# Expert outputs stored to device memory and fetched by row, in place of one-hot combining matmuls

## What is computed

```python
gate, idx = jax.lax.top_k(probs, 2)                    # S = 192 tokens of a group, E = 8
dispatch = jax.nn.one_hot(prio_se, C)                   # C = 60 places for each expert
combine = dispatch * gate_se[..., None]
expert_in = jnp.einsum('gsec,gsd->egcd', dispatch, xg)
h = jax.nn.relu(jnp.einsum('egcd,edf->egcf', expert_in, wi))
expert_out = jnp.einsum('egcf,efd->egcd', h, wo)
out = jnp.einsum('gsec,egcd->gsd', combine, expert_out)
```

## Time and profile before

| | us |
|---|---|
| median of 3 runs | 406.63 (405.19 to 407.81) |
| the profiled execution, its own time | 405.3 |
| its span in the trace | 403.2 |
| TensorE busy | 377.6 (94%) |
| VectorE busy | 196.0 (49%) |
| ScalarE busy | 113.8 (28%) |
| GpSimd busy | 36.7 (9%) |
| window read for the expert stage | 164.0 to 292.8 |

### The profile page before, as it was taken

The page is one execution under the profiler, slowest core; times in us unless marked ns, Lnnn a source line. Parts: engine busy times, 40 slices in busy tenths (PEclk is TensorE's granted clock), DMA queues, the critical chain, the costliest instruction groups (busy, mean ns, idle before and its releaser), DMA issues. The chain is left out here.

```text
span 403.2 us, 8731 instructions
## 1 busy us (share of the span) xinstructions
PE 377.6 (94%) x3760; PEld 269.6 (67%) x3760; DVE 196.0 (49%) x550; ACT 113.8 (28%) x220; POOL 36.7 (9%) x76
## 2 busy tenths in 40 slices
PE   4999999999979998999999999999999999897874
PEld 4989877887867532747566474655776766676574
DVE  4857798765944371114223132302153547967653
ACT  1213245565520333231413213031103123232130
POOL 7002230111020010000000000000011111110100
PEclk9998999999995999999999999999999999996868
DMA  7936960000000000031230303000000000000004
GB/s 283 312 80 200 246 147 2 6 4 3 2 3 0 0 2 0 2 117 29 91 89 30 118 2 119 0 2 0 2 2 0 2 2 1 2 2 2 1 0 117
DMA packets 13426, 20.35 MB, mean 50 GB/s; under 512 B 2954, under 2 KB 9580, under 8 KB 13388
## 3 DMA queue, kind: packets, MB, share of 16 engines
q1 hardware_dynamic: 13388, 19.80, 17.0%
HBM read 18.61 MB, written 1.18 MB: 49 GB/s over the span
## 5 line engine op out<-in xcount | busy, mean ns | idle before, releaser
L604 PE MATMUL banks<-sb_wo_sl,sb_attn_hidT_attn 128*60 128x192 f32 x768 | 64.1, 327 | 0.0
L604 PEld LDWEIGHTS banks<-sb_wo_sl,sb_attn_hidT_attn 128*60 128x60 f32 x768 | 52.9, 133 | 10.8 <-issue 2.4
L1059 ACT ACTIVATE sb_attn_hidT_attn<-banks 128x480 f32<-128x480 f32 x48 | 24.8, 568 | 99.9 <-PE banks L590 99.9
L1493 DVE COPY sb_w_tok_e_out<-banks 60x384 f32<-60x384 f32 x32 | 17.8, 555 | 71.5 <-PE banks L604 71.0
L586 PE MATMUL banks<-sb_tok_xeT,sb_wi_sl 128*128 128x480 f32 x96 | 45.1, 592 | 1.1 <-ACT sb_tok_xeT L1051 1.1
L586 PEld LDWEIGHTS banks<-sb_tok_xeT,sb_wi_sl 128*128 128x128 f32 x96 | 16.3, 189 | 25.4 <-issue 23.5
L1483 DVE TENSOR_TENSOR sb_comb<-sb_cst,sb_slot_of 128x480 f32<-128x480 f32 x12 | 7.8, 654 | 39.4 <-PE banks L219 39.4
L414 PE MATMUL banks<-sb_tok_xeT 128*128 128x193 f32 (+1 forms) x128 | 26.0, 353 | 0.0
L590 PE MATMUL banks<-sb_tok_xeT,sb_wi_sl 64*128 64x480 f32 x96 | 25.8, 615 | 0.0
L414 PEld LDWEIGHTS banks<-sb_tok_xeT 128*128 128x128 f32 (+1 forms) x128 | 22.3, 201 | 3.0 <-issue 2.6
L571 PE MATMUL banks<-sb_onehot_combT,sb_xn 64*64 64x480 f32 (+1 forms) x144 | 21.8, 586 | 0.0
(11 more groups left out here) (203 smaller groups left out, 572.0 us busy)
## 6 DMA issues: line engine op xcount, KB each, us to landing
sb_wo_sl<-in_wo SPq DMA_DIRECT2D x8, 576.0 KB, 4.9
sb_tok_xeT<-in_xin SPq DMA_DIRECT2D x8, 448.0 KB, 6.8
sb_wi_sl<-in_wi SPq DMA_DIRECT2D x8, 288.0 KB, 3.2
sb_wi_sl<-in_wi SPq DMA_DIRECT2D x24, 96.0 KB, 3.2
...
out<-sb_h SPq DMA_DIRECT2D x16, 72.0 KB, 1.8
...
```

The lines of the kernel that those rows point to most:

```text
L604: mm = nc.tensor.matmul(PS[64 * z:64 * z + CAP, 4 + hf, pr * D:(pr + 1) * D], hidT[:, e % 2, f, g * CAP:(g + 1) * CAP], wo_sl[:, q, f], st ...
L1059: nc.scalar.activation(hidT[:, e % 2, f], PS[:, HID_BANKS[(e * (FT // 2) + f // 2) % 2][f % 2], 0:SLOTS], ACT.Relu).then_inc(sem("hidT"), 1)
L1493: ve.tensor_copy(e_out[64 * (e % 2):64 * (e % 2) + CAP, hf * 4 + z:hf * 4 + z + 3:2, e // 2], PS[64 * z:64 * z + CAP, 4 + hf, 0:2 * D].rea ...
```

## The change

The outputs of expert e now go from PSUM to a two-deep SBUF buffer `rows_out`, and SP stores each half to a device memory tensor (`store_rows`, 16 stores of 192 KB). VectorE computes for each token and each of its two choices k the number of the row in that tensor (`find_rows`, 5 operations on up to 192 values a partition; a token that found no place gets a row of zeros). GpSimd waits for the stores and issues 24 indirect DMAs (`fetch_rows`), one for each tile and k, which each bring 128 rows of 768 bytes. VectorE's new `add_experts(j)` adds row times gate to `h`, 6 operations of 128x192 for a group in place of two. All combine tiles, their transposes and copies, and all of `combine` are gone, and with them the waits of later steps on the combining banks. The gates are now one value for each choice. The constant part of the row numbers comes from 8 small memsets on GpSimd at the start.

```diff
-        gate_of = sb("gate_of", [128, TILES, E])
-        turn_space = sb("onehot_combT", [128, TILES * E // 2 * 128])
-        onehot = turn_space[:, 0:2 * NB * E * CAP].rearrange("t (q b s) -> t q b s", q=2, b=NB)
-        combT = turn_space[:].rearrange("s (i e t) -> s i e t", i=TILES, e=E // 2)
-        comb = sb("comb", [128, 2, E, PADCAP])
+        places = sb("places", [128, TILES, 2, E])
+        gate_of = sb("gate_of", [128, TILES, 2])
+        row_e = sb("row_e", [128, 2, 2 * TILES, E])
+        row_f = sb("row_f", [128, 2, 2 * TILES])
+        row_of = sb("row_of", [128, 2 * TILES], U32)
+        row_space = sb("onehot_rows", [128, 2 * TILES * D + 8 * D])
+        onehot = row_space[:, 0:2 * NB * E * CAP].rearrange("t (q b s) -> t q b s", q=2, b=NB)
+        rows_in = row_space[:, 0:2 * TILES * D].rearrange("t (i d) -> t i d", i=2 * TILES)
+        rows_out = row_space[:, 2 * TILES * D:].rearrange("s (q h g d) -> s q h g d", q=2, h=2, g=2)
...
-        e_out = w_space[:].rearrange("s (g e) d -> s g e d", g=PAIRS)
+
+        expert_rows = [nc.dram_tensor(f"expert_rows{hf}", [E * 2 * 128, D], F32).ap() for hf in range(2)]
...
+            def store_rows(e, hf):
+                sp.wait_ge(sem("e_out"), 4 * e + 2 * hf + 2)
+                sp.dma_start(expert_rows[hf].rearrange("(e s g) d -> e s (g d)", e=E, g=2)[E - 1 - e], rows_out[:, e % 2, hf].rearrange("s g d -> s (g d)")
+                             ).then_inc(sem(f"rows_out{e % 2}{hf}"), 16)
+
+            for e in range(NW):
+                load_expert(e)
             for e in range(E):
-                load_expert(e)
+                if e + NW < E:
+                    load_expert(e + NW)
+                store_rows(e, 0)
+                store_rows(e, 1)
...
-            gp.wait_ge(sem("eo_ps"), 2 * E)
+
+            def fetch_rows(j):
+
+                for i in range(NB * j, NB * j + NB):
+                    for k in range(2):
+                        gp.indirect_dma_start(rows_in[:, 2 * i + k], None, expert_rows[j // 2],
+                                              bass.IndirectOffsetOnAxis(ap=row_of[:, 2 * i + k:2 * i + k + 1], axis=0)
+                                              ).then_inc(sem(f"rows_in{i}"), 16)
+
+            gp.wait_ge(sem("row_of"), 1)
+            for hf in range(2):
+                for q in range(2):
+                    gp.wait_ge(sem(f"rows_out{q}{hf}"), 16 * E // 2)
+                for j in range(2 * hf, 2 * hf + 2):
+                    fetch_rows(j)
             gp.memset(o1T[HD:HD + 1, 0], 1.0).then_inc(sem("pads_zero"), 1)
             gp.wait_ge(sem("pads_zero"), 2)
...
-            def turn_comb(i):
-                pe.wait_ge(sem("comb"), i + 1)
-                need(pe, "combT", i - 1)
-                for ep in range(E // 2):
-                    mm = flip(PS[:, 6 + i % 2, ep * 128:(ep + 1) * 128], comb[:, i % 2, 2 * ep:2 * ep + 2].rearrange("t e c -> t (e c)"))
-                mm.then_inc(sem("combT_ps"), 1)
-
-            def combine(j, part):
-
-                if j == 0:
-                    pe.wait_ge(sem("combT"), TILES)
-                elif j > 1:
-                    pe.wait_ge(sem("moe_h"), 2 * j - 1 + part)
-                if (j, part) == (3, 1):
-                    pe.wait_ge(sem("b_knorm"), 1)
-                for blk in ((0, 1), (2,))[part]:
-                    for ep in range(E // 2):
-                        if j == 0:
-                            pe.wait_ge(sem("e_out"), 8 * ep + 8)
-                        for hf in range(2):
-                            rows = slice(64 * hf, 64 * hf + 64)
-                            mm = nc.tensor.matmul(PS[rows, comb_bank(j, part), blk % 2 * D:(blk % 2 + 1) * D],
-                                                  combT[:, NB * j + blk, ep, rows], e_out[:, 2 * j + hf, ep],
-                                                  start=(ep == 0), stop=(ep == E // 2 - 1), skip_group_check=True)
-                mm.then_inc(sem("moe_ps"), 1)
...
             for e in range(E):
                 expert_inner(e)
-                if 0 < e < 7:
-                    turn_comb(2 * e - 2)
-                    turn_comb(2 * e - 1)
                 expert_outer(e)
 
             pe.wait_ge(sem("layer1_in"), 16 * LAYER1_DMAS)
-            combine(0, 0)
-            combine(0, 1)
-            combine(1, 0)
-            combine(1, 1)
+            pe.wait_ge(sem("e_out"), 4 * E)
             turn_linear(0)
-            combine(2, 0)
             linear_keys_values(0, 0)
             linear_queries(0)
             linear_keys_values(0, 1)
             linear_keys_values(0, 2)
             turn_linear(1)
-            combine(2, 1)
             key_products(0)
             key_sums(0)
-            combine(3, 0)
             linear_keys_values(1, 0)
             linear_keys_values(1, 1)
             linear_keys_values(1, 2)
             linear_outputs(0)
-            combine(3, 1)
             key_products(1)
             key_sums(1)
             linear_queries(1)
...
+            def find_rows():
+
+                every = places[:].rearrange("t i k e -> t (i k) e")
+                rev = const("rev").unsqueeze(1).to_broadcast([128, 2 * TILES, E])
+                ve.wait_ge(sem("pads_zero"), 1)
+                ve.tensor_scalar(row_e[:, 0], every, CAP + 1.0, 2.0, ALU.min, ALU.mult).then_inc(sem("row_step"), 1)
+                ve.scalar_tensor_tensor(row_e[:, 1], choice[:].rearrange("t i (k e) -> t (i k) e", k=2), 2 * 128.0, rev,
+                                        ALU.mult, ALU.mult).then_inc(sem("row_step"), 1)
+                ve.wait_ge(sem("row_step"), 2)
+                ve.tensor_tensor(row_e[:, 0], row_e[:, 0], row_e[:, 1], ALU.add).then_inc(sem("row_step"), 1)
+                ve.wait_ge(sem("row_step"), 3)
+                ve.tensor_reduce(row_f[:, 0], row_e[:, 0], AX_X, ALU.add).then_inc(sem("row_step"), 1)
+                ve.wait_ge(sem("row_step"), 4)
+                ve.tensor_tensor(row_of[:], row_f[:, 0], row_f[:, 1], ALU.add).then_inc(sem("row_of"), 1)
...
-            def build_comb(i):
-                need(ve, "combT_ps", i - 1)
-                if i == 0:
-                    ve.wait_ge(sem("pads_zero"), 1)
-                cm = comb[:, i % 2, :, 0:CAP]
-                ve.tensor_tensor(cm, iota, slots_of(i), ALU.is_equal).then_inc(sem("comb_hot"), 1)
-                ve.wait_ge(sem("comb_hot"), i + 1)
-                ve.tensor_tensor(cm, cm, gate_of[:, i].unsqueeze(2).to_broadcast([128, E, CAP]), ALU.mult).then_inc(sem("comb"), 1)
-
             def keep_expert(e):
                 if e == 0:
                     ve.wait_ge(sem("pads_zero"), 1)
                 for hf in range(2):
                     ve.wait_ge(sem("eo_ps"), 2 * e + hf + 1)
+                    need(ve, f"rows_out{e % 2}{hf}", 16 * (e // 2))
                     for z in range(2):
-                        ve.tensor_copy(e_out[64 * (e % 2):64 * (e % 2) + CAP, hf * 4 + z:hf * 4 + z + 3:2, e // 2],
+                        ve.tensor_copy(rows_out[64 * z:64 * z + CAP, e % 2, hf],
                                        PS[64 * z:64 * z + CAP, 4 + hf, 0:2 * D].rearrange("s (g d) -> s g d", g=2)
                                        ).then_inc(sem("e_out"), 1)
 
 
-            def add_experts(j, part):
-                ve.wait_ge(sem("moe_ps"), 2 * j + part + 1)
-                if part == 0:
-                    ve.tensor_tensor(h[:, j, 0:2], h[:, j, 0:2],
-                                     PS[:, comb_bank(j, 0), 0:2 * D].rearrange("t (b d) -> t b d", b=2), ALU.add
-                                     ).then_inc(sem("moe_h"), 1)
-                else:
-                    ve.tensor_tensor(h[:, j, 2], h[:, j, 2], PS[:, comb_bank(j, 1), 0:D], ALU.add).then_inc(sem("moe_h"), 1)
+            def add_experts(j):
+                for k in range(2):
+                    for blk in range(NB):
+                        i = NB * j + blk
+                        if k == 0:
+                            ve.wait_ge(sem(f"rows_in{i}"), 32)
+                        else:
+                            ve.wait_ge(sem("moe_h"), 2 * NB * j + blk + 1)
+                        ve.scalar_tensor_tensor(h[:, j, blk], rows_in[:, 2 * i + k], gate_of[:, i, k:k + 1], h[:, j, blk],
+                                                ALU.mult, ALU.add).then_inc(sem("moe_h"), 1)
...
-            build_comb(0)
-            build_comb(1)
+            find_rows()
             for e in range(E):
                 keep_expert(e)
-                if e < 5:
-                    build_comb(2 * e + 2)
-                    build_comb(2 * e + 3)
-            add_experts(0, 0)
-            add_experts(0, 1)
+            add_experts(0)
             linear_moments(0)
             linear_norm(0)
-            add_experts(1, 0)
-            add_experts(1, 1)
+            add_experts(1)
             linear_moments(1)
             linear_norm(1)
-            add_experts(2, 0)
+            add_experts(2)
             query_norms(0)
```

(3 more changed lines are left out.)

39 lines of the change are left out of this document (16 added, 23 removed).

## The result

| | before | after |
|---|---|---|
| median of the runs, us | 406.7 (4 runs, 405.19 to 407.81) | 423.54 (4 runs, 419.35 to 427.55) |
| ratio, with its 95% interval | | 1.039 [1.032, 1.046] |
| profiled execution, us | 405.3 | 427.55 |
| its span | 403.2 | 425.7 |

The change makes the kernel 16.8 us slower; 13.1 were forecast.

The account below looks back on a forecast made before the run. TensorE was taken to bound the expert stage, then the wait for data behind it. Transposes -6.1, common point -11.2 + 24c, clock +4 give -13.3 + 24c; with c = 1.1, +13.1 us, so 419.7 us, range 407 to 437.

Parts of the forecast that it names:

- What is removed: TensorE's combine transposes, 6.1 us in the expert stage, and combining matmuls, 16.9 us; up to 23.0 us leave TensorE.
- The start of GpSimd: After the last expert: 2.3 us from the first half's copy-out at 290.14 to GpSimd's first fetch at 292.4.
- the sum: Whole kernel: -6.1 transposes, -11.2 + 24c at the common point, +4 clock, together -13.3 + 24c, or +13.1 us.
- The form of the price: Ahead of the linear layer: 24 issues on GpSimd's queue, c us each, then 1.7 us, hold back the first normalization.
- Its size, c: GpSimd's time to issue one indirect DMA, taken as 1.1 us, the middle of computed operations of 0.88 and 1.38.
- the common point: Start of `linear_queries(1)`, at 327.22 us before, forecast at 316.0 + 24c; from there the programs are the same.
- From the normalization to the common point: Linear layer up to `linear_queries(1)`: 21.9 us, before 27.05; of 8.4 us of combining only 5.1 are gained.
- The clock: After TensorE's stop of about 28 us its clock falls to the lower level, costing 4 us in the linear layer.
- Cheap issue: Rival on GpSimd's queue: c is 0.32 to 0.60, 401.0 to 407.7 us; chance 0.06 faster, 0.12 for c 0.38 to 0.72.
- One at a time: Rival on GpSimd's queue: each indirect DMA holds it until landing, c 1.5 to 1.8 or above, 429.3 to 436.5 us; chance 0.16.

Follow-up runs that it names:

- before without transposes: The kernel before without its 24 combine-tile transposes on TensorE and ScalarE's copies of them; 395.92 us, ratio 0.974 to before.
- the first with plain loads: Groups 0, 1 combined by matmuls, 2, 3 fetched and added later; nine of twelve indirect DMAs replaced by SP's plain DMAs after the second scale; 403.14 us.
- the fetches apart: Groups 0, 1 combined by matmuls, 2, 3 fetched and added later; last six fetches wait for group 0's key products; 401.75 us, ratio 0.997 to before.

## Why the prediction was right, point by point

**What is removed.** Right. The expert stage is 6.1 us shorter, as worked out, in after and in before without transposes.

**The start of GpSimd.** 0.9 us short. From the copy's end at 285.78 to the first issue at 288.94 it is 3.16 us, where 2.3 were taken. The store was issued at 285.82 and landed 2.2 us later, as taken. The other 0.9 lie between its landing and the first indirect DMA, which the sum left out. What fills them is not shown.

**The form of the price.** Right. The gap is filled by the issues, the normalization starts 1.8 us behind the last of them (1.7 forecast), and VectorE is idle after six additions. 0, 12 and 24 fetches give 6.34, 17.74 and 32.98 us.

**Its size, c.** This is the term that was mis-sized most: 1.25 us where 1.1 was taken, and with the slower first one 30.2 us in place of 26.4. The busy time, 0.95, does lie between the 0.88 and 1.38 of the computed operations in the earlier trace rows. What was missed are the 0.30 us between two issues. But 1.1 was taken from an analogy, the making of 128 addresses from 128 values, and no run shows that this is what the 0.95 us are spent on; 64 addresses cost 0.90. That the figure came so near is luck in part. Nor does SP's 0.60 us speak for it, as the prediction has it: that is the recorded length of an issue, not the time until a first byte moves. With 1.25, the recorded sum is -13.3 + 30.0 = +16.7 us, where the medians differ by 16.8.

That agreement is closer than the parts deserve. In the profiled executions, the stretch from the last outer product to the common point grew by 23.4 us where 19.2 were forecast, clock included: +3.8 for the issues, +0.9 for the start, +0.1 for the scale, -0.5 behind the normalization. The half-level clock adds 1.7 us behind the common point (queries 4.49 against 2.79 in the earlier trace rows), for which nothing was forecast. By these the change costs 23.4 - 6.1 + 1.7 = 19.0 us in this execution; the interval of the ratio is 12.9 to 18.6. The 2 us between are not accounted for.

**From the normalization to the common point.** The length is right: 25.4 us, against 21.9 and 4 for the clock. Without the 3.4 us that the clock cost it is 22.0, so of the 8.4 us of combining 5.1 were gained and 3.3 turned into waits, as forecast. The waits are where they were walked to be, 0.94 and 0.97 for ScalarE's copies, 0.73 and 0.72 for `own_heads`. One reason was not: `own_heads` was to be held by VectorE's additions, but VectorE stood idle for 0.60 us ahead of it, waiting for TensorE's key products:

```profile
336.33 0.95 DVE L1545 TENSOR_TENSOR sb_attn_hidT_attn<-banks,sb_cst 96x768 f32<-96x768 f32 x1 [0.60 <-PE banks L678]
```

**The clock.** It fell as said, and rows give 1.4 us for the first keys and values, 1.4 for the queries and 0.6 for the transposes in this stretch, 3.4 where 4 were taken; with the 1.7 behind the common point it is 5.1. Its cause was told too simply. Behind stops of 6.34 and 4.93 us, and behind waits of 1.04 and 1.50 us after 30.8 us of dense matmuls, it was as low. And with the same waits ahead to 0.01 us, in two kernels that differ in one wait on SP, 12 matmuls of keys and values took 7.46 us in the first with plain loads and 4.11 in the second; with the fetches apart they took 5.80. So neither the length of the last wait nor the long stop decides it alone, and what does is open.

**The rivals.** *Cheap issue* is refuted by the pitch. Landing does overlap the next issue (2.6 us against 1.25), but an issue takes a fixed 0.95 us for 128 rows and 0.90 for 64. The Trainium skill, "DMA: Bandwidth & Descriptors", section "Anatomy of one DMA", calls descriptor generation small and variable. The part that grows with the rows is small here too, 0.05 us for 64 of them; but the fixed part, by an estimate from these two 0.85 us, holds GpSimd in each instruction, so an issue as a whole is not cheap, and the measurement decides. *One at a time* is refuted by the same overlap, and by a pitch below 1.5 us.
